# Sixteen heads in one instruction: squares, sums of squares and normalised products of 1024 columns

## What is computed

```python
def l2norm(t):
    return t / jnp.maximum(jnp.linalg.norm(t, axis=-1, keepdims=True), 1e-12)

def attn_layer(x, Wqkv, qs, ksc, Wo):
    qkv = x @ Wqkv                       # 128 -> 3 * 1024
    q, k, v = jnp.split(qkv, 3, -1)
    q, k, v = (sh(q), sh(k), sh(v))      # 16 heads of 64
    q = l2norm(q) * qs
    k = l2norm(k) * ksc
    q = q * cos * scale + rotate_half(q) * sin * scale
    k = k * cos * inv + rotate_half(k) * sin * inv
    out = local_attention(q, k, v)       # windows of 32 tokens, each sees itself and the one before
    return out.transpose(0, 2, 1, 3).reshape(b, n, INNER) @ Wo
```

## Time and profile before

| | |
|---|---|
| median of 3 runs | 3211.26 us (3197.78 to 3216.28) |
| the profiled execution | 3208.65 us |
| its span, first to last instruction | 3206.9 us |
| TensorE busy | 2818.5 us (88%) |
| VectorE busy | 2625.2 us (82%) |
| ScalarE busy | 2195.8 us (68%) |
| GpSimd busy | 1374.1 us (43%) |

### The profile page before, as it was taken

How to read it: one execution, slowest core, us unless ns; L and a number is a source line. 1 busy time by engine, 2 the same in 40 slices (tenths; PEclk the granted TensorE clock), 3 DMA queues, 4 the chain that set the end, 5 groups by cost and what they waited for, 6 DMA issues and landing times. The chain is left out here.

```text
span 3206.9 us, 74211 instructions
## 1 busy us (share of the span) xinstructions
PE 2818.5 (88%) x29085; PEld 1571.1 (49%) x29181; DVE 2625.2 (82%) x3842; ACT 2195.8 (68%) x3490; POOL 1374.1 (43%) x818
## 2 busy tenths in 40 slices
PE   3999998998988889789988998998899889988998
PEld 1233333333433333356746663666367646755764
DVE  4999889888788689379868986998689778978995
ACT  2377677677656667678857875887588668856884
POOL 0200433425224210166636663666366546645661
PEclk8699999999989999899999999999999999999999
DMA  3200001010010210011111110111011111111110
GB/s 112 66 2 2 1 8 31 8 31 1 9 31 2 47 40 2 11 41 35 35 43 39 37 55 16 41 41 51 26 35 38 52 28 35 37 46 34 34 41 21
DMA packets 62990, 101.14 MB, mean 32 GB/s; under 512 B 20450, under 2 KB 45216, under 8 KB 61472
## 3 DMA queue, kind: packets, MB, share of 16 engines
q1 hardware_dynamic: 62636, 96.26, 10.9%
HBM read 38.30 MB, written 7.34 MB: 14 GB/s over the span
## 5 line engine op out<-in xcount | busy, mean ns | idle before, releaser
L916 DVE TENSOR_REDUCE a_part<-ps 128x1 f32<-128x512 f32 (+3 forms) x1664 | 986.1, 653 | 168.2 <-PE ps L594 161.4
L892 ACT ACTIVATE a_Pb<-ps 128x1024 f32<-128x1024 f32 (+3 forms) x832 | 762.8, 974 | 357.9 <-PE ps L760 356.6
L1271 PE MATMUL ps<-early 128*128 128x512 f32 x1152 | 564.2, 624 | 99.3 <-DVE l_qn L1649 71.1
L1208 POOL TENSOR_TENSOR l_sine<-l_qn,stack 128x512 f32<-128x512 f32 x192 | 344.5, 1794 | 253.6 <-DVE l_qn L1649 246.1
L1232 POOL TENSOR_TENSOR l_weights<-l_weights,l_rcp 128x1024 f32<-128x1024 f32 x96 | 182.5, 1901 | 476.2 <-DVE l_rcp L1686 476.2
L594 PE MATMUL ps<-stack,a_QS 48*128 48x512 bf16 x1024 | 314.3, 409 | 74.7 <-DMA a_QS<-pieces 32.8
L1271 PEld LDWEIGHTS ps<-early 128*128 128x128 f32 x1152 | 206.2, 193 | 328.6 <-issue 153.2
L1638 DVE TENSOR_REDUCE l_norm<-l_square 128x8 f32<-128x512 f32 x384 | 252.5, 679 | 106.2 <-ACT l_square L1484 92.3
L1484 ACT ACTIVATE l_square<-ps 128x512 f32<-128x512 f32 x384 | 228.3, 597 | 107.0 <-PE ps L1271 102.8
L1649 DVE TENSOR_TENSOR l_qn<-ps,l_norm 128x512 f32<-128x512 f32 x384 | 246.5, 684 | 63.8 <-ACT l_norm L1494 60.1
L1657 DVE TENSOR_TENSOR l_cosine<-l_qn,stack 128x1024 f32<-128x1024 f32 x192 | 279.8, 1457 | 4.1
(11 more groups left out here) (217 smaller groups left out, 5051.7 us busy)
## 6 DMA issues: line engine op xcount, KB each, us to landing
l_V_earlier<-l_V SPq DMA_DIRECT2D x96, 384.0 KB, 3.5
l_V_earlier<-l_V SPq DMA_DIRECT2D x96, 128.0 KB, 3.3
early<-in_L_ffn_Wqkv_dram SPq DMA_DIRECT2D x6, 1536.0 KB, 8.4
a_QS<-pieces SPq DMA_DIRECT2D x96, 64.0 KB
pieces<-a_piece SPq DMA_DIRECT2D x6, 512.0 KB, 2.6
pieces<-early SPq DMA_DIRECT2D x12, 256.0 KB, 2.7
a_KS<-pieces SPq DMA_DIRECT2D x48, 64.0 KB
l_w_o<-in_L_ffn_Wo_dram SPq DMA_DIRECT2D x6, 512.0 KB, 4.0
```

Of the source, the lines that this page charges most:

```text
L892: e.activation(Pb[:, n % 2, 2 * p:2 * p + 2, lo:CH], ps[:, 2 * p:2 * p + 2, lo:CH], ACT.Exp)\
L916: e.tensor_reduce(part[:, u % 2, column(h, qt), b:b + 1], bank[:, 0:width], AX.X, ALU.max)\
L1208: e.tensor_tensor(sine[:, :, 0:ROT], swap[:, :, ROT:LD], table[:, :, 0:ROT], ALU.mult).then_inc(s.rotated, 1)
L1271: e.matmul(ps[:, (V_BANK[T] if i == 2 else 0) + b, :], XS[:, T * P:(T + 1) * P], w_qkv[:, at:at + CH], start=True, stop=True).then_inc(s.v ...
```

## The change

Squares, sums of squares and the normalised products are made for all 16 heads at once: one instruction of 1024 columns, over both PSUM banks where PSUM is read, in place of two of 512. The semaphores `square`, `total` and `qn` count one for a Q or a K where they counted two, and the waits on them are rewritten accordingly. Where a half waited for a half, the whole now waits for the whole: the square for both halves of the projection, each half of the next projection for the whole of `normalise`. No instruction stands in another order.

```diff
 rotate (POOL):
-                    e.wait_ge(s.qn, 2 * n + 2)
+                    e.wait_ge(s.qn, n + 1)
 project (TensorE):
-                        e.wait_ge(s.qn, 2 * (2 * n + i) - 1 + b)
+                        e.wait_ge(s.qn, 2 * n + i)
...
-                def squares(l, T, i, b):
+                def squares(l, T, i):
                     n = (l * NT + T) * 2 + i
-                    e.wait_ge(s.a_ready, START + (l * NT + T) * 4 + 2 * i + b + 1)
-                    if b == 0:
-                        e.wait_ge(s.total, START + 2 * n)
-                    e.activation(square[:, HALF * b:HALF * (b + 1), :].rearrange("p h d -> p (h d)"), ps[:, b, :], ACT.Square)\
-                        .then_inc(s.square, 1)
+                    e.wait_ge(s.a_ready, START + 2 * n + 2)
+                    e.wait_ge(s.total, START + n)
+                    e.activation(square[:, :, :].rearrange("p h d -> p (h d)"), flat2(ps[:, 0:2, :]), ACT.Square).then_inc(s.square, 1)
 
                 def inverse_norms(l, T, i):
                     n = (l * NT + T) * 2 + i
-                    e.wait_ge(s.total, START + 2 * n + 2)
+                    e.wait_ge(s.total, START + n + 1)
...
                 def sum_squares(l, T, i):
                     n = (l * NT + T) * 2 + i
-                    for b in range(2):
-                        heads = slice(HALF * b, HALF * (b + 1))
-                        e.wait_ge(s.square, 2 * n + b + 1)
-                        e.tensor_reduce(norm[:, 0, heads], square[:, heads, :], AX.X, ALU.add).then_inc(s.total, 1)
+                    e.wait_ge(s.square, n + 1)
+                    e.tensor_reduce(norm[:, 0, :], square[:, :, :], AX.X, ALU.add).then_inc(s.total, 1)
 
                 def normalise(l, T, i):
...
-                    for b in range(2):
-                        heads = slice(HALF * b, HALF * (b + 1))
-                        e.tensor_tensor(qn[:, i, heads, :], ps[:, b, :].rearrange("p (h d) -> p h d", h=HALF),
-                                        norm[:, 2, heads].unsqueeze(2).to_broadcast([P, HALF, LD]), ALU.mult).then_inc(s.qn, 1)
+                    e.tensor_tensor(qn[:, i, :, :], by_head(flat2(ps[:, 0:2, :])),
+                                    norm[:, 2, :].unsqueeze(2).to_broadcast([P, LH, LD]), ALU.mult).then_inc(s.qn, 1)
...
```

More of the change, by code:

```diff
@@ L1356, in mean @@
                     if c == 0:
-                        e.wait_ge(s.qn, (l + 1) * (4 * NT))
+                        e.wait_ge(s.qn, (l + 1) * (2 * NT))
                     if c == 2:
@@ L1555, in attend @@
                         if T == 0:
-                            squares(l, 1, 0, 0)
-                            squares(l, 1, 0, 1)
+                            squares(l, 1, 0)
                             inverse_norms(l, 1, 0)
@@ L1561, in attend @@
                         if ahead:
-                            squares(l, T + 1, 1, 0)
-                            squares(l, T + 1, 1, 1)
+                            squares(l, T + 1, 1)
                         if T:
@@ L1573, in attend @@
                         if T + 2 < NT:
-                            squares(l, T + 2, 0, 0)
-                            squares(l, T + 2, 0, 1)
+                            squares(l, T + 2, 0)
                         exponentials(l, T)
@@ L1606, in forward @@
                             e.preload_act_table_set(LN_EXP)
-                            for b in range(2):
-                                squares(l + 1, 0, c - (NC - 2), b)
+                            squares(l + 1, 0, c - (NC - 2))
                             inverse_norms(l + 1, 0, c - (NC - 2))
@@ L1614, in _ @@
                 for i in range(2):
-                    for b in range(2):
-                        squares(0, 0, i, b)
+                    squares(0, 0, i)
                     inverse_norms(0, 0, i)
```

## The result

The changed kernel takes 3389.28 us (median of 4 runs, 3385.55 to 3396.14), the kernel before 3206.18 us in the runs beside it (3197.78 to 3216.28). The ratio is 1.058 with a 95% interval of 1.0555 to 1.0604: some 183 us slower, where 149 were forecast. The time lies inside the range and in its upper half. The profiled execution of the changed kernel has a span of 3383.8 us, 176.9 more than before.

What follows compares the result with a forecast made beforehand. Bound: a chain round the engines, shortened by handing over halves. Steady tiles 140.3 us, layer changes 4.6 and opening 3.9 sum to 148.8 us more than 3208.65: 3357 us, range of 8 in 10 3300 to 3405.

Steps and rivals of the forecast that it cites:

- The bound: In a steady tile, a chain of normalise, project, square, sum, inverse norm, twice a tile, sets the 15.33 us.
- K's chain: From normalise Q through K's projection, square and sum to normalise K: 1.08 us later in a steady tile.
- The savings: Merged pairs save some 0.06 us each on DVE, 0.25 us a tile, and 0.19 us twice a tile on ACT.
- The wait of the values for ACT's weights: The second half of the values on TensorE waits 0.30 us for L1530, which stands behind the inverse norm on ACT.
- Q's chain: From Q's projection, starting at 8.84 instead of 8.10, to the next normalise Q at 17.00: 1.67 us more a tile.
- The walk: Steady tile followed link by link from normalise Q: 17.00 us in place of 15.33; chance 0.77.
- The edges: Outside the 14 steady tiles of each layer: 4.6 us between layers, 3.9 us at the opening, nothing at the last tiles.
- The rival of the start costs: Fewer instructions pay on DVE: 0.25 us saved in all 96 tiles, 24 us faster, 3185 us; chance 0.03.
- Only K's chain: TensorE's 0.74 us delay finds cover, so a tile costs about 0.93 to 1.08 us more: 3301 us; chance 0.09.
- The clock: Longer TensorE idle slows K's projection by 1.80 us: 151 us if every tile, 15 if one in ten; chance 0.08.

Runs made afterwards that it cites:

- the sums alone: Only the sum of squares made one instruction of 1024 columns, squares and products in halves, against the kernel before: ratio 1.017.
- the squares alone: Only the square made one instruction of 1024 columns, sums and products in halves, against the kernel before: ratio 1.0449.
- the kernel with whole waits: The kernel before, instructions still halves of 512 columns, but each step waiting for both halves of the step ahead: ratio 1.077, 3455.76 us.
- the kernel before with the cosines moved: The kernel before, in halves, with the cosines of K made ahead of the sums of Q's squares on DVE: ratio 1.0033.

## Why the prediction was right, and where it was short

- **The bound** was read rightly: a chain round the engines, through the very steps that are changed, seen in two short waits of DVE. That Q's wait was not slack is shown by the sums alone (0.53 us a tile). K's chain had a little room: in the same run normalise K comes 0.15 us later, and Q's projection still starts 8.10 us behind normalise Q.
- **The savings** came as forecast (1.22 us for 1.27 and 1.29 on DVE, 1.02 for 1.19 on ACT). They count, but they are small: against the same waits in halves the large forms save 0.41 us a tile (17.60 to 17.19), and the waits alone cost 2.27 (15.33 to 17.60). The square was taken as 1.00 us; this is 0.02 of the miss in each chain.
- **K's chain** was forecast 1.08 us late and is 1.11 late. The wait of the values for ACT's weights, a knock-on that no row of before showed, is there: it was worked out from two rows of different engines.
- **Q's chain** is the term that was too small: 1.67 us a tile became 1.86. Q's projection comes 0.09 us later than forecast. The walk had taken 0.1 us off K's projection, for a second half that no longer waits for its own half of Q; but the projection takes 1.99 us after and 1.98 before, so there was nothing to take off. The square starts 2.10 us behind Q's projection in place of 2.02, which the trace does not explain, and takes 0.02 more. The three errors of the walk add up because all lie on one chain: 0.19 us, some 15 us in 78 steady tiles.
- **The edges** were forecast at 8.5 us and came out otherwise. This is where the two profiled executions differ, counted from one L1677 (L1666 after) to the next:

  | stretch | forecast, us | measured, us |
  |---|---|---|
  | ahead of the layers' first projection | 0 | -7.8 |
  | the opening | 3.9 | 6.3 |
  | the first tile of each layer | 10.0 | 21.0 |
  | 13 steady tiles of each layer | 130.3 | 150.4 |
  | the last tile of each layer | 0 | -6.0 |
  | the five stretches from layer to layer | 4.6 | 13.5 |
  | behind the last of them | 0 | -0.5 |
  | sum | 148.8 | 176.9 |

  The first tile grew by 3.5 us on the mean (14.2 to 17.7), where the walk has 1.67. In five of the six layers K's projection there is at the lower clock (3.3 to 3.8 us, 3.78 in the fifth); in the second it is not, and the tile still grew by 2.5 us. From layer to layer the walk has 0.93 us, for Q alone, and the trace 2.7; the squares alone add 4.2 there and the sums alone 1.6, so K's part, which was put at nothing, is a likely place, but no run separates it. The steady tiles' miss is Q's 0.19 us and the long tiles' 9 us. The part ahead of the layers is the same in all the kernels and took between 1345 and 1359 us in their profiled executions; that it was 7.8 us shorter here hides so much of the miss, by luck.
- **The rival of the start costs** is out: no part alone is faster. The Trainium skill's rule on which it drew (VectorE: DVE Perf Modes, section "The TRN2 errata — SBUF-src ops pay a fixed extra latency per instruction") holds for the engine's own time of the sums, which read SBUF, 234.1 us in place of 252.5, and did not decide the total.
- **Only K's chain** is out: TensorE found no cover for its delay. Q's projection starts 8.93 us behind normalise Q where it started at 8.10, and the wait ahead of Q's sum alone was worth two thirds of the loss.
- **The clock** was forecast as a rival of its own, with 15 us for one tile in ten. Some 9 us in the steady tiles came, and a part of the first tiles' growth: it is a part of the loss, not a case beside the others. The Trainium skill tells of such a swing behind short idle times (TensorE: Matmul & The Clock Gate, section "A second HAM failure mode: psum-queue depth-cycling"); the trace of the kernel with whole waits agrees, with projections of 1.98 and 3.49 us behind the same idle times.

## What to carry to other kernels

Where one engine hands its result to the next, two halves can cost a little more on each engine and much less on the way: the second half of one step runs beside the first half of the next. Here the large forms save 0.41 us a tile and the lost handing over costs 2.27. Before merging, look who waits for the instruction: if the idle time ahead of it, or ahead of what reads it, is near zero or ended by the step before in the same chain, the merged form lengthens the chain at each hand-over. Where the engine is bound by its own work and its reader comes late anyway, merging should pay; no run here has that case. Where a wait has to stay, independent work that stands behind it in the same queue may go ahead of it, if one looks at what is queued behind the work that is pushed back, and at what runs on the other engines when the moved work starts.

## What the runs showed of the hardware

TensorE's clock can fall behind short idle times. In the kernel with whole waits, idle times of 0.77 and 1.5 us, with 1.09 us of transposes between them, ended with K's projection at 3.3 to 3.8 us in some three steady tiles of ten and at 1.98 us in the others. With eight more transposes there, and 0.64 us of idle time ahead of the projection, none of the steady tiles was struck. What decides which tile is struck is not shown.

A product on DVE with both inputs in SBUF (the cosines, 128x1024) takes 1.22 us where no product of GpSimd's runs as it starts. When it starts while one of GpSimd's products runs, it ends 1.08 us behind the end of that product: in all 90 such cases of the kernel before and in all 174, to 0.01 us, of the kernel before with the cosines moved. So 1.22 became 1.76 or 1.88 us, and up to 1.96. It looks as if the one waits for the other; no run takes GpSimd's products away.

The last of the six layers, which runs outside the loop, has shorter tiles than the five inside it, in every kernel: 15.16 us against 15.33 before, 16.95 against 17.19 after. The work is the same. Inside the loop the values that the waits compare with are worked out in registers; that this is the cause is argued only, and was not tried.
